# Local attention in blocks of 32 queries, norms by ScalarE's square root, PSUM slots by due time

## The reference

```python
def local_attention(q, k, v):            # q, k, v: (b, 16, 256, 64), w = 32
    ...                                  
    bk2, bv2 = (look(bk), look(bv))      
    mask = (it < jb) | (it > jb + w) | (jb == -1)
    sim = jnp.einsum('bhwie,bhwje->bhwij', bq, bk2) * QK_SCALE
    sim = jnp.where(mask, -jnp.finfo(sim.dtype).max, sim)
    attn = jax.nn.softmax(sim, -1)
    out = jnp.einsum('bhwij,bhwje->bhwie', attn, bv2)
    return out.reshape(b, h, n, d)

def attn_layer(x, Wqkv, qs, ksc, Wo):
    ...
    q = l2norm(q) * qs
    k = l2norm(k) * ksc
    ...
    q = q * cos * scale + rotate_half(q) * sin * scale
    k = k * cos * inv + rotate_half(k) * sin * inv
    out = local_attention(q, k, v)
    return out @ Wo

def ffn_layer(x, g, bln, W1, b1, W2, b2):
    ...
    a, gate = jnp.split(hg, 2, -1)
    return a * jax.nn.gelu(gate, approximate=False) @ W2 + b2
for i in range(DEPTH):                   # DEPTH = 6
    x = attn_layer(shift_tokens(x), ...) + x
    x = ffn_layer(shift_tokens(x), ...) + x
```

## Time and profile before

| | us |
|---|---|
| median of the runs | 4593.13 |
| profiled execution: span from first to last instruction | 4596.8 |
| TensorE matmuls busy | 4085.1 (89%) |
| VectorE busy | 3862.2 (84%) |
| GpSimd busy | 3640.7 (79%) |
| ScalarE busy | 3501.9 (76%) |

### The profile page before, as it was taken

One profiled execution on the slowest core, in us unless ns is written; L12 is line 12 of the kernel. 1 busy time (PEld: TensorE's weight loads), 2 busy tenths in 40 slices (PEclk: granted clock), 3 DMA queues, 4 the chain that ended last, 5 costly groups with the idle time before them and its releaser, 6 DMA issues.

```text
span 4596.8 us, 140828 instructions
## 1 busy us (share of the span) xinstructions
PE 4085.1 (89%) x57664; PEld 3035.9 (66%) x57664; DVE 3862.2 (84%) x6471; ACT 3501.9 (76%) x6378; POOL 3640.7 (79%) x2624
## 2 busy tenths in 40 slices
PE   7987466557885999999999999999999999999997
PEld 5665345445663667776777767776777777777776
DVE  4664999864555989998999989998999989999994
ACT  4664788874543778887888888887888878888885
POOL 1111888863337999998999999998999999999994
PEclk9999788888997999999999999999999999999999
DMA  2000000000000222222222222222222222222222
GB/s 64 2 2 1 1 1 1 1 1 28 2 2 8 53 55 54 64 66 57 56 60 73 54 61 54 64 69 55 57 59 73 54 61 54 64 70 59 55 58 62
DMA packets 120845, 198.83 MB, mean 43 GB/s; under 512 B 66896, under 2 KB 78224, under 8 KB 120080
## 3 DMA queue, kind: packets, MB, share of 16 engines
q1 hardware_dynamic: 120208, 189.82, 16.7%
HBM read 24.12 MB, written 2.10 MB: 6 GB/s over the span
## 4 chain that ended last, share of the span: by engine, by line
PE 61%; DVE 13%; POOL 12%; issue 8%; ACT 5%; DMA 0%; DVEq 0%; POOLq 0%; SPq 0%; ACTq 0%
PE ps L1306 7%; PE ps L1250 7%; PE ps L1251 6%; PE ps L1317 6%; PE ps L1278 4%; PE ps L1297 3%; PE ps L1290 3%; PE ps L1358 3%; PE ps L1298 3%; POOL arena L1585 3%; POOL arena L1590 2%; PE ps L1347 2%; PE ps L1341 2%; PE ps L1259 2%; DVE arena L1512 2%
## 5 line engine op out<-in xcount | busy, mean ns | idle before, releaser
L1585 POOL TENSOR_TENSOR arena<-arena 128x32 f32<-128x32 f32 x192 | 1138.8, 5931 | 72.3 <-DVE arena L1498 72.3
L1590 POOL TENSOR_TENSOR arena<-arena 128x1024 f32<-128x1024 f32 x384 | 907.1, 2362 | 11.0 <-DVE arena L1489 10.9
L208 POOL TENSOR_SCALAR arena<-arena 128x2 f32<-128x2 f32 x256 | 72.5, 283 | 645.6 <-DVE arena L202 634.4
L1376 ACT ACTIVATE arena<-ps 128x1024 f32<-128x1024 f32 x384 | 391.1, 1021 | 198.3 <-PE ps L1251 193.3
L1488 DVE TENSOR_TENSOR arena<-ps,arena 128x1024 f32<-128x1024 f32 x384 | 468.5, 1220 | 79.6 <-ACT arena L1376 73.3
L1608 POOL TENSOR_TENSOR arena<-arena 128x1536 f32<-128x1536 f32 x192 | 529.0, 2755 | 1.8 <-DVE arena L1522 1.8
L1489 DVE TENSOR_TENSOR arena<-ps,arena 128x1024 f32<-128x1024 f32 x384 | 466.5, 1215 | 0.0
L1306 PEld LDWEIGHTS ps<-arena 96*64 96x64 f32 x12288 | 385.4, 138 | 115.5 <-issue 115.3
L1496 DVE TENSOR_REDUCE arena<-arena 128x32 f32<-128x2048 f32 x192 | 437.0, 2276 | 0.0
L1250 PE MATMUL ps<-arena 128*128 128x512 f32 x768 | 414.5, 622 | 18.4 <-DVE arena L1514 15.8
L1397 ACT ACTIVATE arena<-arena 128x96 f32<-128x96 f32 x1536 | 427.1, 368 | 2.4 <-DVE arena L1514 2.4
(11 more groups left out here) (252 smaller groups left out, 9793.2 us busy)
## 6 DMA issues: line engine op xcount, KB each, us to landing
arena<-arena SPq DMA_DIRECT2D x192, 384.0 KB, 4.3
arena<-arena SPq DMA_DIRECT2D x192, 256.0 KB, 3.7
arena<-arena SPq DMA_DIRECT2D x192, 128.0 KB, 2.3
arena<-in_dWqkv SPq DMA_DIRECT2D x18, 512.0 KB, 3.6
arena<-arena SPq DMA_DIRECT2D x96, 64.0 KB
arena<-arena SPq DMA_DIRECT2D x96, 63.5 KB
arena<-in_dWo SPq DMA_DIRECT2D x6, 512.0 KB, 5.8
arena<-in_x SPq DMA_DIRECT2D x4, 512.0 KB, 7.4
```

Source lines behind the costliest of these rows:

```text
L1585: pool.tensor_tensor(ss[:, 0:32], ss[:, 32:64], mhalf32, ALU.pow).then_inc(*S.rs.up())
L1590: pool.tensor_tensor(a1[:, half], a1[:, half], T2[:, half], ALU.add).then_inc(*radd[g].up())
```

## The change

Only `phase_d` changes, with its constants and the layout of its weights.

- A block is 32 queries and 64 keys. `s` is one piece per tile: eight mask matmuls of 512 columns, and 64 float32 matmuls (128 instructions) with 32 output rows and 64 columns, on two row halves and four column quarters of the array. `mx`, `ex` and `sum` are one piece each over 1024 columns.
- `p` is 16 transposes of 64 rows x 128 columns (two heads at once), and `PT`, now double, holds 128 rows. `o` is 64 float32 matmuls (128 instructions) with 64 rows of contraction, 64 output rows and 32 columns. Half of the blocks of v are read from `VN` (three buffers) as they lie, the others from `VW`, which eight DMAs fill. The heads of v and of `Wo` are reordered on the host side.
- The norms: VectorE takes the reciprocal of the sums, ScalarE the square root (`rt`), and GpSimd scales all of q and k (`nrm0`, `nrm1`, 1024 columns each). `rs`, VectorE's `nrm1`, the scaled exponentials and `mhalf32` go.
- `Slots` replaces `Banks`: a use takes the slot whose last reader is due first.
- All due times are new. SyncE loads `b1` in a piece `lb1` of its own.

```diff
     def before(self, use):
         i = self.place[use] - self.n
         return self.uses[i] if i >= 0 else None
+
+
+class Slots:
+
+
+    def __init__(self, n):
+        self.last, self.until, self.place, self.prev = [None] * n, [-1e9] * n, {}, {}
+
+    def take(self, use, until):
+        i = self.until.index(min(self.until))
+        self.place[use], self.prev[use] = i, self.last[i]
+        self.last[i], self.until[i] = use, until
+
+    def slot(self, use):
+        return self.place[use]
+
...
-    V = [sb([96, 2, 1024]) for _ in range(2)]
-    PP = [sb([128, 16, 96]) for _ in range(3)]
-    VN = [sb([128, 1024]) for _ in range(2)]
-    PT = sb([96, 16, 128])
+    PP = [sb([128, 16, 64]) for _ in range(3)]
+    VN = [sb([128, 1024]) for _ in range(3)]
+    VW = [sb([128, 3, 512]) for _ in range(2)]
+    PT = [sb([128, 1024]) for _ in range(2)]
...
-    TILE = {"q0": 454, "q1": 501, "sq0": 591, "ro0": 633, "sq1": 639, "ro1": 824, "ssum": 1063, "radd0": 1067,
-            "rs": 1496, "radd1": 1632, "halo": 2028, "t0": 2112, "nrm1": 2153, "t1": 2245, "nrm0": 2269, "qT": 2438,
-            "kT": 2489, "s0": 3069, "mx0": 3289, "s1": 3363, "mx1": 3485, "ex0": 3540, "ex1": 3855, "sum": 4371,
-            "v": 5691, "vn": 5765, "vd": 5865, "pn": 5954, "p0": 6001, "p1": 6029, "pT0": 6239, "pT1": 6249,
-            "o": 6646, "oT": 6735, "wo": 6903, "xxa": 7120}
-    BATCH = {"sh": 0, "xs": 155, "fd": 10386, "fst": 12271, "fn": 14710, "frs": 14881, "ft": 14904, "fzT": 15078,
-             "fg": 15528, "fge": 15704, "fa": 15822, "fgm": 16094, "fo": 16318, "xxf": 16393}
-    LAYER = {"tab": 16000, "lqk": 31551, "lv": 36771, "lwo": 38053, "lw1": 45922, "lw2": 46518}
-    EDGE = {"e0": 18323, "e1": 19383, "e2": 21333, "e3": 21383, "out": 23753}
+    TILE = {"q0": 1283, "radd0": 1529, "q1": 1595, "sq0": 1624, "radd1": 1638, "nrm0": 1685, "ro0": 1762,
+            "sq1": 1784, "ro1": 2006, "nrm1": 2241, "ssum": 2264, "halo": 2369, "rt": 2764, "t0": 2940, "t1": 3134,
+            "qT": 3212, "kT": 3484, "s": 3935, "mx": 4252, "sum": 4408, "ex": 4478, "pn": 4500, "v": 4796,
+            "vn": 4989, "vd": 5089, "p": 5602, "PT": 5920, "o": 6006, "oT": 6312, "wo": 7094, "xxa": 7336}
+    BATCH = {"sh": 0, "xs": 239, "fd": 8386, "frs": 8454, "fst": 8935, "fn": 10940, "ft": 12520, "fzT": 12732,
+             "fg": 12861, "fa": 13177, "fge": 13197, "fgm": 13341, "fo": 18630, "xxf": 18896}
+    LAYER = {"tab": 16000, "lqk": 32695, "lv": 35896, "lwo": 38194, "lw1": 43277, "lb1": 43391, "lw2": 48830}
+    EDGE = {"e0": 20796, "e1": 21896, "e2": 23796, "e3": 23846, "out": 26196}
...
+    frees = {"sh": "xs", "q0": "ro0", "q1": "ro1", "t0": "qT", "t1": "kT", "s": "mx", "p": "PT", "v": "vn", "o": "oT",
+             "wo": "xxa", "ft": "fzT", "fg": "fge", "fa": "fgm", "fo": "xxf"}
+    bufs = Slots(4)
...
+        if piece in frees and piece in TILE:
+            bufs.take((piece, l * NT + k), 1000 * (l * NT + k) + TILE[frees[piece]])
+        if piece in frees and piece in BATCH:
+            bufs.take((piece, l * NB + k), 1000 * (l * NT + 2 * k) + BATCH[frees[piece]])
...
+            if piece == "s":
+                pe.wait_ge(*S.qT.at(n + 1))
+                pe.wait_ge(*S.kT.at(n + 1))
+                pe.wait_ge(*S.halo.at(n + 1))
+                qT, kT, p = QT[n % 2], KT[n % NKT], claim("s", n)
+                for blk in range(4):
                     for bank in range(2):
                         half = slice(64 * bank, 64 * bank + 64)
-                        pe.matmul(p[64 * blk:64 * blk + 64, 512 * bank:512 * bank + 384], identb[half, half],
-                                  maskd[half, 1 if k % 2 or blk else 0, :], start=True, stop=False, skip_group_check=True)
-                for j in range(4):
-                    for blk in range(2):
+                        pe.matmul(p[32 * blk:32 * blk + 32, 512 * bank:512 * bank + 512].rearrange("p (c k) -> p c k", c=8),
+                                  identb[half, 64 * bank:64 * bank + 32], bc(maskd[half, 1 if k % 2 or blk else 0, :], 1, 8),
+                                  start=True, stop=False, skip_group_check=True)
+                for c in range(8):
+                    for blk in range(4):
                         for bank in range(2):
-                            rows = slice(64 * bank, 64 * bank + 64)
-                            i = pe.matmul(p[64 * blk:64 * blk + 64, 512 * bank + 96 * j:512 * bank + 96 * j + 96],
-                                          qT[rows, 4 * g + j, 64 * blk:64 * blk + 64],
-                                          kT[rows, 4 * g + j, 64 * blk:64 * blk + 96],
+                            half = slice(64 * bank, 64 * bank + 64)
+                            i = pe.matmul(p[32 * blk:32 * blk + 32, 512 * bank + 64 * c:512 * bank + 64 * c + 64],
+                                          qT[half, c, 32 * blk:32 * blk + 32], kT[half, c, 32 * blk:32 * blk + 64],
                                           start=False, stop=False, skip_group_check=True)
-                i.then_inc(*s_ps[g].up())
-            if piece in ("p0", "p1"):
-                g = int(piece[1])
+                i.then_inc(*S.s_ps.up())
+            if piece == "p":
                 pe.wait_ge(*S.pn.at(n + 1))
...
+                p, P = claim("p", n), PP[n % 3].rearrange("p x k -> p (x k)")
+                for c in range(8):
+                    for rows in range(2):
+                        half = slice(64 * rows, 64 * rows + 64)
+                        i = pe.transpose(p[:, 512 * rows + 64 * c:512 * rows + 64 * c + 64], P[half, 128 * c:128 * c + 128],
                                          ident[half, half])
-                i.then_inc(*p_ps[g].up())
+                i.then_inc(*S.p_ps.up())
...
+                pe.wait_ge(*S.PT.at(n + 1))
+                pe.wait_ge(*s_v[n % 2].at(128 * (n // 2 + 1)))
+                p, pT, vn, vw = claim("o", n), PT[n % 2], VN[n % 3], VW[n % 2]
+                for e in range(4):
+                    for blk in range(4):
+                        for c in (2 * e, 2 * e + 1):
+                            for u in range(2):
+                                half = slice(64 * u, 64 * u + 64)
+                                if blk == (1, 3)[u]:
+                                    v = vn[half, 512 * u + 64 * c:512 * u + 64 * c + 64]
+                                else:
+                                    v = vw[half, ((0, 0, 1, 2), (0, 1, 2, 2))[u][blk], 64 * c:64 * c + 64]
+                                q0 = 512 * (blk // 2) + 64 * c + 32 * (blk % 2)
+                                i = pe.matmul(p[64 * (c % 2):64 * (c % 2) + 64, 512 * u + 128 * e + 32 * blk:512 * u + 128 * e + 32 * blk + 32],
+                                              v, pT[half, q0:q0 + 32], start=True, stop=True, skip_group_check=True)
...
+            if piece == "rt":
+                if n >= 3:
+                    act.wait_ge(*S.nrm_q.at(n - 2))
+                    act.wait_ge(*S.nrm_k.at(n - 2))
+                act.wait_ge(*S.ssum.at(n + 1))
+                act.activation(SS[n % 3][:, 0:32], SS[n % 3][:, 32:64], ACT.Sqrt).then_inc(*S.rt.up())
+            if piece == "ex":
+                P = PP[n % 3]
+                act.wait_ge(*S.sub.at(n + 1))
+                act.activation(P, P, ACT.Exp).then_inc(*S.ex.up())
+            if piece == "PT":
+                if n >= 2:
+                    act.wait_ge(*S.o_ps.at(n - 1))
+                act.wait_ge(*S.p_ps.at(n + 1))
+                act.activation(PT[n % 2], ps("p", n), ACT.Copy).then_inc(*S.PT.up())
             if piece == "vn":
+                if n >= 3:
+                    act.wait_ge(*S.o_ps.at(n - 2))
+                    act.wait_ge(*s_v[(n - 3) % 2].at(128 * ((n - 3) // 2 + 1)))
                 if n >= 2:
-                    act.wait_ge(*(S.v1 if n % 2 else S.v0).at(48 * (n // 2)))
-                if n:
-                    act.wait_ge(*(S.v0 if n % 2 else S.v1).at(48 * ((n - 1) // 2 + 1)))
+                    act.wait_ge(*s_v[(n - 2) % 2].at(128 * ((n - 2) // 2 + 1)))
                 act.wait_ge(*S.v_ps.at(n + 1))
-                act.activation(VN[n % 2], ps("v", n), ACT.Copy).then_inc(*S.vn.up())
+                act.activation(VN[n % 3], ps("v", n), ACT.Copy).then_inc(*S.vn.up())
...
+                dve.tensor_scalar(ss[:, 32:64], ss[:, 32:64], 1e-24, None, ALU.max).then_inc(*S.step_dve.up())
+                dve.wait_ge(*S.step_dve.now())
+                dve.reciprocal(ss[:, 32:64], ss[:, 32:64]).then_inc(*S.ssum.up())
+            if piece == "mx":
...
+                    dve.wait_ge(*S.p_ps.at(n - 2))
+                pv = ps("s", n).rearrange("p (x k) -> p x k", x=16)
+                dve.wait_ge(*S.s_ps.at(n + 1))
+                dve.tensor_reduce(mx, pv, AX.X, ALU.max).then_inc(*S.step_dve.up())
                 dve.wait_ge(*S.step_dve.now())
-                dve.tensor_tensor(Pg, pv, bc(mg, 3, 96), ALU.subtract).then_inc(*sub[g].up())
```

(33 more changed lines are left out.)

123 lines of the change are left out of this document (31 added, 92 removed).

## The result

The changed kernel takes 4916.3 us (4910.5 to 4922.4) against 4593.3 us: ratio 1.0701, 95% interval 1.0686 to 1.0717. The forecast was 4444, the range ended at 4590: wrong in sign and far outside. The profiled execution spans 4909.1 us.

What follows compares the result with a forecast made beforehand. It took TensorE's back-to-back work to bound the kernel: 4596.8 + 96 x (-1.7 on TensorE + 0.2 for waits) - 5 at layer borders = 4448 us of span, 4444 as the runs' median; range 4245 to 4590.

Steps and rivals of the forecast that it cites:

- Scores: TensorE's masks and score matmuls, eight side by side: 1.25 us per tile, 1.3 us saved per batch.
- The same limit doesn't touch the scores: Score weights of 32 columns load in 27 ns, below 54 ns of streaming, so weight loads don't limit them.
- Transposes: TensorE's transposes of the probabilities: 16 instead of 32 per tile, 0.65 us instead of 1.03, 0.76 saved per batch.
- `o`: TensorE's attention output: loads of 64-column weights take some 58 ns per matmul in each quarter, so no change in time.
- Order: TensorE's new piece order: separate entries for `t0` and `t1` +0.3 us per batch, splitting `q0` from `q1` at most 0.1.
- Other engines: GpSimd 23.3, VectorE 24.6 and ScalarE 25.8 us per batch, all fitting under TensorE's new period of 30.0.
- that rival: ScalarE's table switches cost about 2.66 us each with a drain; 32.7 us per batch, about 4700 us; chance 3%.
- (a): Norm's longer way through VectorE, ScalarE and GpSimd to `t0` fits with about 0.8 us; 0.2 per batch charged with slots.
- (b): Four PSUM slots all held just before `s`, the first free some tenths ahead; 0.2 us per batch charged with the norm.
- (c): SyncE's eight value copies per tile instead of three cost nothing, as `o` comes a whole tile (15 us) after its `v`.
- (d): GpSimd's 8.5 us wait at each of five layer borders stays; its new slack gives back 5 us in all.
- number of matmuls: Small matmuls on TensorE stay at 20.6 ns each, so scores and output take 5.0 us more per batch: 4925; chance 11%.

Runs made afterwards that it cites:

- x1: Separate kernel with only TensorE streams of float32 matmuls, no computation: new output's matmuls 14.5 ns apart, new scores' 9.9, between stops.
- x2: Changed kernel with `o` and its copy due later, so that `q0` runs ahead of `o`; same instructions: 4802.6 us, ratio 1.0451.
- x10: Changed kernel with `o` and its copy due later, ScalarE's first square earlier and VectorE's 1e-24 floor as a tensor_reduce: 4497.5 us, ratio 0.9785.
- x6: Changed kernel with VectorE's floor of 1e-24 on the sums of squares left out: 4907.1 us, ratio 1.0677.
- x3: Kernel before with the norm part alone: reciprocal, root on ScalarE, both scalings on GpSimd, whole exponentials: 4858.6 us, ratio 1.0566.
- x4: Changed kernel with PSUM slots handed out in turn again (`Banks` instead of `Slots`): 5234.2 us, ratio 1.1370.

## Why the prediction was wrong, point by point

- *The bound* was read rightly: TensorE, with nothing to gain from the others. The rest of the sum worked from durations and asked only what the array does with a matmul; it had no term for how fast instructions reach it.
- *Scores*: 1.25 us a tile forecast, 1.74 measured in the mean (1.62 to 1.96). The first 16 matmuls do run eight side by side at 56 ns, then they come every 10 to 12 ns: +1.0 us per batch, so 0.3 saved instead of 1.3. The step took an eight-way rate from a four-way one. "The same limit doesn't touch the scores" fell: x1 has them at 9.9 ns where the moved columns alone ask for 54/8 = 6.8.
- *Transposes* (0.64, forecast 0.65) and *`o`* without a standstill (2.07, forecast 2.06) were right. That something other than the moved columns binds `o` is shown by x1 (14.5 ns, where they ask for 27/4 = 6.8); that it is the load of wide weights stays unproven.
- *Order*: `o` right behind `t0` and the scores was priced by its entries, +0.4 us per batch. That is the step that failed: the supply of instructions was put at nothing without a reason, and it cost the standstills, +3.3, and with them the clock, +1.5. x1 shows the limit by itself; x2 and x10, with the same instructions on TensorE in another order, show that the order decides what it costs. These 4.8 and the 1.0 of the scores outweigh the 1.7 that was forecast as gain.
- *Other engines*: from the stretch's seven batches (14 tiles), GpSimd 22.7 us per batch (forecast 23.3), ScalarE 25.9 (25.8), with 35 table loads of 1.28 us in seven batches and no drain, so that rival is out. VectorE 27.0 against 24.6, of which 2 x 0.78 us are the floor's waiting for GpSimd.
- *Waits*: (a) the norm's way had a wait that no row of before showed, since the floor there mostly met the end of GpSimd's instruction or none; in after it is covered (x6), on the old kernel it isn't (x3). (b) No slot wait, true, but only by the slots' new rule (x4). (c) Not nothing: 72 us. (d) "It stays" was wrong: between 1700 and 4450 us before waits 28 us for GpSimd at four layer borders, after none.
- *Rivals*: "number of matmuls" gave 4925, 9 us from the result, and that the cost comes from how many there are was right. That the number fits so well is luck: it charged 3.5 us per batch to the scores and 1.6 to `o` at 20.6 ns each, where the scores took 1.0 and no matmul has such a fixed time (8.5 to 14.5 ns occur). Its sign, `o` at 2.8 us, didn't come either: `o` runs in 2.07 and stands still beside it. The limit is 3.5 us or more per 256 instructions, once those fetched ahead are used up. The count of instructions, 57664 to 79168, and the 462 packets of the instruction queue stood in the page of before and in the diff.

## What to carry to other kernels

Count instructions, not only columns. Where TensorE gets through 256 instructions in less than about 3.5 us and goes on so, it stands still once those fetched ahead are used up; in x1 that was after 183 to 291 pairs. The remedy is order: wide matmuls between narrow pieces gave 114 us by themselves. With the floor's new form and the earlier square, +7% became -2%. An edit's worth depends on what else is late: leaving out the floor was worth 9 us, 88 us or 180 us in three surroundings. A small VectorE instruction on a dependent chain beside a busy GpSimd should be of a form that doesn't wait for it.

## What the runs showed of the hardware

- TensorE gets 256 instructions (16 KB) per 3.5 to 4.0 us when it is starved, whether they are 1.3 or 2.9 us of work (x1). Behind wide matmuls a dense stream runs on for 183 to 291 pairs before its first stop.
- A tensor_scalar of 32 elements lasted 1.6 us in the mean beside GpSimd's 1.9 us scalings, a tensor_reduce and a reciprocal of the same size 0.22 and 0.35.
- Every stretch of the clock's lower level in after comes shortly after TensorE stood idle for 0.9 us or more, but most such idle times have no low clock behind them: 242 us of 2850 with 247 us of standstills (after), 15 with 46 (x10).
- Between standstills, fp32 matmuls with 32 moved columns start 14.5 ns apart with 64-column weights on four parts of the array, and 8.5 ns apart with 32-column weights on eight (x1).
